# Stacked attentions: masked keys placed by transfers through DRAM, input rows normalised on GpSimd, routing in other slots

## The reference, cut to what matters

```python
x = x + L0_xattn(layernorm(x), ctx);  x = x + L0_ffn(layernorm(x))      # routed low-rank experts
x = x + L1_xattn(layernorm(x), ctx);  x = x + L1_ffn(layernorm(x))      # shared and routed experts
x = x + L2_xattn(layernorm(x), ctx);  x = x + L2_ffn(layernorm(x))      # top-2 of 8, with capacity
x = x + L3_xattn(layernorm(x), ctx);  x = x + L3_ffn(layernorm(x))      # a whole block: own attention, then experts
# every attention, 16 heads of width 8:
q, k, v = h @ Wq, c @ Wk, c @ Wv          # c is ctx (120 keys) or, in L3_ffn, h itself (128 keys)
out = softmax(q k^T / sqrt(8) + mask) v @ Wo
# L2_ffn: expert of each token by top-2 of h @ wg; its place in the expert's table by a running count
```

## Time and profile before

| | us |
|---|---|
| median of 3 runs (lowest, highest) | 4146.7 (4140.27, 4158.86) |
| the profiled execution, its own time | 4131.01 |
| its span, first to last instruction | 4128.9 |
| busy in the span: PE, DVE, ACT, POOL | 3458.1, 3417.6, 2382.1, 1545.5 |
| mean granted clock of PE | 0.909 of full |

### The profile page before, as it was taken

One profiled execution on the slowest core, in us unless ns is written; L12 is line 12 of the kernel. 1 busy time (PEld: TensorE's weight loads), 2 busy tenths in 40 slices (PEclk: granted clock), 3 DMA queues, 4 the chain that ended last, 5 costly groups with the idle time before them and its releaser, 6 DMA issues. The chain is left out here.

```text
span 4128.9 us, 95016 instructions
## 1 busy us (share of the span) xinstructions
PE 3458.1 (84%) x31907; PEld 2505.8 (61%) x31907; DVE 3417.6 (83%) x6484; ACT 2382.1 (58%) x4440; POOL 1545.5 (37%) x935
## 2 busy tenths in 40 slices
PE   6983979998599788888568839989499998899999
PEld 3553647766477465565456627667366666677777
DVE  7888879999799788878755579889788888788888
ACT  2431657776277466655545527667576665466665
POOL 1210035553000345555444435545155563122222
PEclk9985989999599899989788969999699998899999
DMA  2001322222100222222121142222222222000000
GB/s 65 14 25 64 130 50 64 66 61 53 42 1 0 50 56 55 60 56 56 52 76 57 58 127 64 59 60 58 64 58 48 53 57 77 24 16 15 15 10 16
DMA packets 161066, 209.96 MB, mean 51 GB/s; under 512 B 38044, under 2 KB 110048, under 8 KB 157857
## 3 DMA queue, kind: packets, MB, share of 16 engines
q1 hardware_dynamic: 151457, 187.83, 16.8%
q0 software_dynamic: 8192, 16.92, 1.2%
q10 hardware_dynamic: 1152, 1.57, 0.2%
HBM read 53.09 MB, written 42.21 MB: 23 GB/s over the span
## 5 line engine op out<-in xcount | busy, mean ns | idle before, releaser
L1102 ACT ACTIVATE a_p<-a_p 128x480 f32<-128x480 f32 x832 | 501.7, 603 | 528.5 <-DVE a_p L939 521.8
L698 POOL TENSOR_TENSOR a_km<-a_k,a_slots 96x1920 fp32r<-96x1920 f32 x186 | 631.3, 3410 | 184.9 <-DMA a_k<-a_kh 181.2
L934 DVE TENSOR_REDUCE a_mx<-a_sc 128x4 f32<-128x480 f32 (+1 forms) x832 | 540.6, 650 | 129.8 <-PE a_sc L1206 106.4
L939 DVE TENSOR_TENSOR a_p<-a_sc,a_mx 128x480 f32<-128x480 f32 x832 | 531.8, 639 | 19.7 <-DVE a_mx L934 0.5
L1108 ACT ACTIVATE a_pt<-a_tp 120x512 f32<-120x512 f32 x832 | 485.4, 584 | 104.0 <-PE a_tp L1215 101.6
L1215 PE MATMUL a_tp<-ident,a_p 128*120 128x128 f32 x3328 | 518.9, 280 | 6.1 <-ACT a_pt L1108 6.1
L1200 PE MATMUL a_sc<-a_km,a_qr 96*128 96x480 f32 x768 | 403.5, 525 | 103.0 <-DVE a_p L939 71.5
L1215 PEld LDWEIGHTS a_tp<-ident,a_p 128*120 128x120 f32 x3328 | 414.7, 141 | 84.8 <-issue 37.2
L1239 PE MATMUL a_nd<-a_pt,a_vm 120*32 120x128 f32 x6656 | 297.6, 285 | 19.2 <-ACT a_pt L1108 18.8
L1200 PEld LDWEIGHTS a_sc<-a_km,a_qr 96*128 96x128 f32 x768 | 149.0, 194 | 210.4 <-issue 116.6
L2196 ACT ACTIVATE f_s<-f_pu 128x512 f32<-128x512 f32 x256 | 153.5, 600 | 212.4 <-PE f_pv L1678 212.4
(11 more groups left out here) (455 smaller groups left out, 8840.3 us busy)
## 6 DMA issues: line engine op xcount, KB each, us to landing
a_qr<-a_qh SPq DMA_DIRECT2D x372, 64.0 KB, 2.0
a_k<-a_kh SPq DMA_DIRECT2D x384, 60.0 KB, 2.0
a_ctx<-in_ctxT SPq DMA_DIRECT2D x64, 240.0 KB, 2.7
a_qr<-a_ql SPq DMA_DIRECT2D x186, 64.0 KB, 2.0
a_k<-a_kl SPq DMA_DIRECT2D x192, 60.0 KB, 2.0
dispatched<-f_empty SPq DMA_DIRECT2D x8, 1040.0 KB, 20.9
f_xr<-dispatched SPq DMA_DIRECT2D x32, 260.0 KB, 2.6
chosen<-f_none SPq DMA_DIRECT2D x8, 1024.0 KB, 11.8
```

Of the source, the lines that this page charges most:

```text
L698: v.tensor_tensor(KM[par][:, i, :, :].rearrange("p b (j k) -> p b j k", k=KN), K3[:, i, :, :].unsqueeze(2).to_broadcast([TR, GB, 4, KN]), ...
L934: v.tensor_reduce(mx[:], view, AX.X, ALU.max).then_inc(mx_ready, 1)
L939: v.tensor_tensor(PR[s % 4][:].rearrange("p (h k) -> p h k", k=k), view, mx[:].unsqueeze(2).to_broadcast([P, heads, k]), ALU.subtract).the ...
L1102: a.activation(PR[s % 4][:], PR[s % 4][:], ACT.Exp).then_inc(exp_ready, 1)
```

## The change

- **Keys.** For all groups but the first, SP writes the high and the low part of the keys to a DRAM tensor (2 transfers), waits until both have landed, and reads them back with 12 transfers straight into the 8 rows by 16 pieces of KM that each head class owns. The pieces are one row of keys long (480 bytes, 512 in `s`). The zeros around them stay: KM[0]'s come from the first group, KM[1]'s from one memset on POOL. K3 and `masked_keys` remain for the first group alone. PE waits for all 12 reads at a group's first slot.
- **Input rows.** `rows(g)` on POOL normalises them, 4 instructions a group; `ln_sequence` on DVE is gone.
- **Programs.** The loops of POOL and SP over groups are written out.
- **Routing.** The same pieces run at other slots; PE gives the bank back between its transposes and its logits; Newton steps are paired in one slot; POOL scatters in two clusters of up to six.

```diff
--- before.py
+++ after.py
@@ -151,10 +151,10 @@
-    def apply_one(self, dve, g, j, h):
+    def apply_one(self, engine, g, j, h):
...
         b = g * GB + j
-        return self.nc.vector.tensor_scalar(h[:, j, :], self.R.x[:, b, :], self.mean[:, bass.ds(b, 1)],
+        return engine.tensor_scalar(h[:, j, :], self.R.x[:, b, :], self.mean[:, bass.ds(b, 1)],
@@ -295,7 +295,7 @@
         self.main_last = None
-        self.uses = [0, 0, 0, 0]
+        self.uses = [0] * 6
@@ -353,7 +353,8 @@
             for n in range(4):
-                yield
+                if n % 2 == 1:
+                    yield
@@ -369,7 +370,7 @@
             L, L2, eq, one = self.L, self.L2, self.eq, self.one
-            yield from self.at("dve", self.GROUPS * b + 3, 13)
+            yield from self.at("dve", self.GROUPS * b + 4, 4)
@@ -398,7 +399,7 @@
             v.tensor_tensor(self.base[1 - b % 2][:], self.base[b % 2][:], self.cnt[:], ALU.add).then_inc(self.base_ready, 1)
-            yield from self.at("dve", self.GROUPS * b + 4, 4)
+            yield from self.at("dve", self.GROUPS * b + 4, 9)
@@ -408,7 +409,7 @@
             done += 3
-            yield from self.at("dve", self.GROUPS * b + 4, 6)
+            yield from self.at("dve", self.GROUPS * b + 4, 10)
@@ -442,7 +443,7 @@
             for g in range(self.GROUPS * b, self.GROUPS * (b + 1)):
-                yield from self.at("dve", g + 4, 10 - 10 * (g % self.GROUPS))
+                yield from self.at("dve", g + 4, 14 - 14 * (g % self.GROUPS))
@@ -461,7 +462,7 @@
                 i = g % self.GROUPS
-                yield from self.at("act", self.GROUPS * b + 3, 7 + 2 * i)
+                yield from self.at("act", self.GROUPS * b + 3, 5 + 7 * i)
@@ -469,23 +470,24 @@
                 last.then_inc(self.lh_ready, 1)
-                yield from self.at("act", self.GROUPS * b + 3, 9 + 2 * i)
+                yield from self.at("act", self.GROUPS * b + 3, 9 + 5 * i)
...
                 a.activation(self.HS[:], self.bank[:], ACT.Copy).then_inc(self.hs_ready, 1)
-                yield
+                self.uses[1] += 1
+                yield from self.at("act", self.GROUPS * b + 3, 11 + 7 * i)
...
                              ACT.Copy).then_inc(self.l_ready, 1)
-                self.uses[1] += 1
-            yield from self.at("act", self.GROUPS * b + 4, 2)
+                self.uses[5] += 1
+            yield from self.at("act", self.GROUPS * b + 4, 8)
...
             for g in range(self.GROUPS * b, self.GROUPS * (b + 1)):
-                yield from self.at("act", g + 4, 5 - 5 * (g % self.GROUPS))
+                yield from self.at("act", g + 4, 10 - 10 * (g % self.GROUPS))
@@ -512,7 +514,7 @@
                 i = g % self.GROUPS
-                yield from self.at("pe", self.GROUPS * b + 3, 9 + 2 * i)
+                yield from self.at("pe", self.GROUPS * b + 3, 10 + 5 * i)
@@ -520,16 +522,20 @@
                 self.uses[0] += 1
-                yield
+                self.held = (self.hs_ready, g + 1)
+                yield from self.at("pe", self.GROUPS * b + 3, 12 + 7 * i)
                 pe.wait_ge(self.hs_ready, g + 1)
+                self.take_bank(pe)
+                self.after_main(pe)
...
                 last.then_inc(self.lg_done, 1)
+                self.uses[4] += 1
                 self.held = (self.l_ready, g + 1)
-            yield from self.at("pe", self.GROUPS * b + 4, 5)
+            yield from self.at("pe", self.GROUPS * b + 4, 10)
@@ -557,7 +563,7 @@
             b, i = g // self.GROUPS, g % self.GROUPS
-            yield from self.at("pool", g + 4, 12 - 12 * i)
+            yield from self.at("pool", g + 4, 14 - 12 * i)
@@ -590,7 +596,6 @@
     TR = 3 * 32
-    LN_SLOTS = (0, 0, 0, 0) if own_keys else (1, 1, 2, 2)
@@ -669,6 +674,7 @@
             q3_in = [sem(n_(f"q3_in{i}")) for i in range(4)]
+            keys_kept, keys_empty, keys_in = (sem(n_(s)) for s in ("keys_kept", "keys_empty", "keys_in"))
@@ -689,6 +695,17 @@
+        def parts_free(eng, step, g):
...
+            if step == "k" and isinstance(g, int) and g == 1:
+                for i in range(4):
+                    eng.wait_ge(k3_in[i], 48)
+            elif step == "k":
+                at_least(eng, keys_kept, 32 * (g - 1))
+            else:
+                for i in range(4):
+                    at_least(eng, q3_in[i], 48 * g)
@@ -754,14 +771,24 @@
+                kept_keys = R.keys[0:2 * P * GB * KN].rearrange("(n q s) -> n q s", n=2, q=32)
...
                     sp.wait_ge(low_ready["k"], g + 1)
-                    for i in range(4):
-                        at_least(sp, km_ready[i], g)
-                        for term, part in enumerate((HIGH, LOW, HIGH)):
-                            sp.dma_start(K3[32 * term:32 * term + 32, i, :, :].rearrange("p b k -> p (b k)"),
-                                         part["k"][32 * i:32 * i + 32, :].bitcast(F32)).then_inc(k3_in[i], 16)
+                    for n, part in enumerate((HIGH, LOW)):
+                        sp.dma_start(kept_keys[n].rearrange("q (i f) -> i q f", i=4),
+                                     part["k"][:].bitcast(F32)).then_inc(keys_kept, 16)
+                    sp.wait_ge(keys_kept, 32 * g)
+                    if par == 1:
+                        sp.wait_ge(keys_empty, 1)
+                    at_least(sp, sc_ready, (g - 1) * S)
+                    for term, n in enumerate((0, 1, 0)):
+                        for j in range(4):
+                            row = 32 * term + 8 * j
+                            sp.dma_start(KM[par][row:row + 8, :, :, j * KN:(j + 1) * KN].bitcast(F32),
+                                         kept_keys[n, 8 * j:8 * j + 8, :].rearrange(
+                                             "r (s k) -> r s k", k=KN)).then_inc(keys_in, 16)
@@ -775,7 +802,7 @@
                 if own_keys:
-                    groups_loop(sp, lambda g, par, first, last: stack_first() if first else stack_terms(g, par), 3)
+                    groups_in_full(lambda g, par, first, last: stack_first() if first else stack_terms(g, par))
@@ -786,15 +813,10 @@
-                def pair(g):
-                    ctx_load(g + 2, 0)
-                    stack_terms(g + 1, 1)
-                    ctx_load(g + 3, 1)
-                    stack_terms(g + 2, 0)
...
-                pairs_loop(sp, NG - 2, pair)
-                stack_terms(NG - 1, 1)
+                for g in range(1, NG):
+                    if g + 1 < NG:
+                        ctx_load(g + 1, (g + 1) % 2)
+                    stack_terms(g, g % 2)
@@ -818,8 +840,7 @@
-                    for i in range(4):
-                        at_least(pool, (k3_in if step == "k" else q3_in)[i], 48 * g)
+                    parts_free(pool, step, g)
@@ -831,17 +852,22 @@
+                def rows(g):
...
+                    at_least(pool, psum_done["ht"], g)
+                    for j in range(GB):
+                        last = norm.apply_one(nc.gpsimd, g, j, H)
+                    last.then_inc(h_ready, 1)
...
                 def prepare(g, par):
+                    if own_keys:
+                        rows(g)
                     low_part("k", g)
-                    masked_keys(pool, nc.gpsimd, g, par, (0,))
-                    scatter(g - 1, 4, 3)
+                    if not own_keys:
+                        rows(g)
+                    scatter(g - 1, 5, 6)
                     low_part("q", g)
-                    masked_keys(pool, nc.gpsimd, g, par, (1,))
-                    scatter(g - 1, 11, 2)
-                    masked_keys(pool, nc.gpsimd, g, par, (2,))
-                    scatter(g - 1, 13, 2)
-                    masked_keys(pool, nc.gpsimd, g, par, (3,))
-                    scatter(g - 1, 15, 3)
+                    scatter(g - 1, 14, 6)
@@ -851,12 +877,12 @@
                 masked_keys(pool, nc.gpsimd, 0, 0, (0, 2))
+                pool.wait_ge(h_ready, 1)
+                nc.gpsimd.memset(KM[1][:].bitcast(F32), 0.0).then_inc(keys_empty, 1)
...
                     scattering = route.pool_side = route.gpsimd(pool)
-                    groups_in_full(group)
-                else:
-                    groups_loop(pool, group)
+                groups_in_full(group)
@@ -889,13 +915,6 @@
-                def ln_sequence(g, j):
...
-                    at_least(dve, psum_done["ht"], g)
-                    ins = norm.apply_one(dve, g, j, H)
-                    if j == GB - 1:
-                        ins.then_inc(h_ready, 1)
@@ -987,8 +1006,6 @@
                     if not last:
-                        if U > 1:
-                            steps += [lambda j=j: ln_sequence(g + 1, j) for j in range(GB) if LN_SLOTS[j] == s]
@@ -1055,8 +1072,7 @@
-                    for i in range(4):
-                        at_least(act, (k3_in if step == "k" else q3_in)[i], 48 * g)
+                    parts_free(act, step, g)
@@ -1187,7 +1203,10 @@
                     if packed and j == 0:
-                        pe.wait_ge(km_ready[i], g + 1)
```

(7 more changed lines are left out.)

## The result

The changed kernel takes **4299.4 us** (4 runs, 4296.5 to 4300.0), the kernel before, run beside it, 4144.2: a ratio of **1.0371** (95% interval 1.0348 to 1.0395). That is 3.7% slower, where the forecast was 4121 us and the range ended at 4200.

What follows compares the result with a forecast made beforehand. PE and DVE were taken to bound a1, PE a3 and s, and waits, many for DVE held up by POOL, a2. 4131.0 - 15 - 54 + 9 + 34 = 4105, plus 15.7 to the runs' median: 4121 us, range 4060 to 4200.

Steps and rivals of the forecast that it cites:

- The keys' way through DRAM: In s, writes, reads and queries on SP's queue make a group 33.0 us in place of 30.65: +34 us.
- W: Time of a group's two key writes to DRAM in s: between 2.9 and 7.3 us, taken as 5.5.
- rival C: Writes with an outermost dimension of 4 take W's upper bound, 7.3 us; s +58, total 4145 us; chance 0.17.
- The reads: In s, issuing 12 takes 8.0 us, then the queries' issue 4.6 and landing 2.0, less 0.9.
- rival B: Reads into 8 partitions in short pieces are slow, 13.6 us for 12; s +85, a1 +21, total 4208; chance 0.20.
- The part ahead of the writes: In s, from a group's first scores until the writes can start: 13.8 us.
- a1: Phase a1: the gain lies half way between PE's 6.6 us wait for DVE and its 19.6 idle: -15 us.
- Hidden, just: In a1 the keys' chain through DRAM ends at 27.9 us at the latest, wanted at 27.4 + 0.9, costing nothing.
- a3: Phase a3: PE, busy for 424.4 of 440 us, is the limit already, so the change brings 0.
- a2: Phase a2: two thirds of the 47.3 us wait for DVE's subtraction and the 20.2 for routing's rows go: -54 us.
- The two signs named: In a2, the routing copies of L450 near their minimum and PE's wait for `rt_hl` gone would show the forecast right.
- Start-up: KM[1]'s memset on POOL delays the second group: +7 us in s, about +2 in the others, +9 in all.

Runs made afterwards that it cites:

- e1: Changed kernel with the two writes of the kept keys laid out in DRAM as 128 rows instead of 4 by 32, reads unchanged; 4202 us.
- e2: Changed kernel with the 12 reads going to an unused tile, still 8 partitions each, in one 8 KB piece a partition; 4276 us.
- e3: Changed kernel with the 12 reads going to an unused tile as 32 partitions of 2 KB each; 4225 us.
- e13: Changed kernel with the edits of e1, e3 and e6 together; 4039 us.
- e11: Changed kernel with the edits of e1 and e6 together; 4100 us.
- e6: Changed kernel with the input rows still on POOL but made a group earlier; 4234 us.
- e5: Changed kernel with the input rows back on DVE, in the slots of the kernel before; 4248 us.
- e7: Changed kernel with PE's program written out in a1 and a3, where it was a loop over pairs of groups; 4204 us.
- e14: Kernel before with PE's program written out in a1 and a3; 4106 us.
- e8: Kernel before with only the routing's new slots and PE's split of the routing as changed; 4139 us.
- e9: Changed kernel run again without any edit, on the same chip as e10; 4252 us.
- e10: Kernel before run again without any edit, on the same chip as e9; 4124 us.

## Why the prediction was wrong, step by step

**The keys' way through DRAM (+34 taken, +134 measured) is the step that failed.** Its place, its chain and what is late (SP's queue, then PE's first slot) were right. Three terms were too small, here by the means of 14 groups:
- W was taken as 5.5 and measured 8.7, above even the upper end of 7.3. That end came from a transfer of 512 KB which used all engines (16 updates of its semaphore); a form with an outermost dimension of 4 was given the middle "because two transfers start together", though rival C named the reason against it. e1 shows the reason: share 0.25 and 8.7 us with 4, share 0.62 and 3.3 us with 128. The rule of the Trainium skill (DMA: Bandwidth & Descriptors, "Why a DMA increments its semaphore by 16 and not by 1") gives the writes 4 of 16 engines; the trace agrees, 0.25 of them busy, at 92 GB/s, which is 23 an engine. At that rate the 512 KB take 5.7 us; the rest of the 8.7 is not split further. The prediction's 4.9 us of data is an estimate from the figure for one engine that the Trainium skill gives (DMA: Bandwidth & Descriptors, Specifications); that figure is about 27 GiB/s, not GB/s, and makes it an estimate of 4.5.
- The reads were taken at SP's issuing, 8.0, with the queries as the end, 13.7 in all; they took 15.4. The transfers whose price was used write 32 partitions; these write 8. e2 and e3 split the price: 1.3 us for the 512-byte pieces, a further 4.3 at least for the 8 partitions. This is rival B's mechanism (36.7 a group); B had the reads right (15.6 against 15.4) and W too low. By the same rule of the Trainium skill the reads run on 8 engines each, and the transfers of e3 on 16; the trace agrees, with 9 updates of the semaphore a read and 16 in e3 (a write on 4 engines has 5). Which 8 they are, and why the DMA share passes one half (0.67), isn't shown.
- The part ahead of the writes took 15.2 instead of 13.8. In the group shown PE's granted clock is 0.50 for the first 5 us, behind the stall. In e13, where PE doesn't wait for keys and the granted clock of s is 0.98 in the mean (0.87 in the changed kernel), this part is 13.1 in most groups, and in e11, which differs from e13 by the reads alone and stalls, 14.3. So some 1.1 us go with the stall and the clock behind it, for which the sum had no term.

5.5 to 8.7, 13.7 to 15.4 and 13.8 to 15.2 are 6.3 us on top of 33.0: 39.3, the mean length of a group.

**a1 (-15 taken, +19 measured).** "Hidden, just" failed twice. The chain through DRAM was worked out with reads of 8.0 and asks for about 29 (29.1 in e6, where PE waits for the queries behind it), what rival B said. And the rows on POOL cost 0.80 us, not 0.33: 3.1 a group, between the keys' low part and PE's turn, 1.4 of wait. Either alone makes a1 28.6 to 29.2 (e1, e5, e6); without both it is 27.4 (e11). Of the -15 not more than 5 was there: with both gone a1 takes 437 us instead of 442. PE's largest wait left is for ACT's copies (10.8 us for `a_pt` in e11; 7.8 before). One reading behind the -15 was wrong as well: the layer norm's 526 ns on DVE in a1 were put down to the masked keys, but with those gone and the rows on DVE (e5) they are still 494.

**a3 (0 taken, +31 measured).** "PE is the end already" was read from the earlier trace rows without its waits: 15.4 us of the stretch of before were three stalls at the edge of PE's loop. The changed kernel has six, 26.4 us; without them it is at 29.3 (e7), the kernel before at 27.9 (e14). The transfers through DRAM don't explain six instead of three: e8 has six (21.7 us) without them. Of the 1.4 a group between these, 1.0 is PE's wait for the rows on POOL (15.7 us in the 440 from 2400 in e7, 15 groups); the rest was not traced.

**a2 (-54 taken; -19 in the profiled pair, -73 on the chip of e9 and e10).** The mechanism was right in that POOL's masked keys held DVE up: L410 above takes 167 ns without them and 3067 with them. The two signs named don't show it, since both appear in e8, where a2 gains little: the copies at L450 (L451 now: median 165, maximum 365 instead of 2093) and the wait for `rt_hl`. In e8 the 21.7 for `a_ct` stand in the place of the 20.2 counted for that wait. That the slots alone would bring nothing was right within 0.6 a group. The amount was missed both times: too large for the profiled pair, too small for the other chip.

**Start-up (+9 taken).** In s PE waits 12.3 us for the first rows instead of 6.1, +6.2 for the +7. In a2 it waits 9.8 for the first subtraction, where it was 5.3: there two DVE instructions in front of it end only with POOL's memset (see below).

## What to carry to other kernels

Price a transfer by the rows of one with the same outermost dimension and the same number of partitions, not of the same size. If there is none, don't trust bounds from other forms: here even the upper one, 7.3, was passed by 8.7. Time it by itself and look at the DMA share meanwhile. A chain that is hidden by less than its least certain term is not hidden, and when two chains end at the same place, undoing either shows nothing: undo both. A change that pays in one phase (a2, whose group has room for the long way) and costs in the others is worth splitting by phase: that was 2% faster than before (with PE's program written out, and on one chip), all of it together 3.7% slower. And a sign that the forecast names should be one that the rivals don't give as well: the quick copies and the lost wait for `rt_hl` came in e8 without the gain.

## What the runs showed of the hardware

- POOL's `tensor_scalar` with two per-partition operands takes 796 ns for 128 elements a partition; its `tensor_tensor` takes 1279 for 512. The cost is not by elements alone.
- POOL's masked keys and a small DVE instruction: 3067 ns at the median with them (e8), 167 without.
- A DMA's semaphore shows how far it was spread: 5 updates a write with an outermost dimension of 4 (92 GB/s), 9 a read into 8 partitions, 16 where it is 32 or 128 (230 GB/s for the writes of e1).
- During POOL's memset of 6.5 us (1421.61 to 1428.10) a `tensor_scalar` of 8 elements on DVE started at 1423.7 and took 4.45 us, to the memset's end; small memsets on DVE started beside it and took 0.07.
- In a3 the first scores behind an edge of PE's loop come 3.4 to 5.4 us late. It isn't at each of the six edges in the kernel before (3 in one execution, 2 in another), it is in the changed one and in e8, whose a3 is that of before, and quick writes don't alter it (27.0 us in e11). What decides it, and why a1, with the same loop, is free of it, stays open.
- The changed kernel's a2 took 599 us in the first trace and 540 in e9, with the same text; the kernel before took 618 and 613. Where the difference comes from stays open.
